# A hybrid layer on one core: the steady batch's steps written out in another order

## The reference

```python
x = x + mixer(layernorm(x))          # RWKV-6: token shift, low-rank mixes, r/w/k/v/gate, a scan over time
x = x + butterfly_ffn(layernorm(x))  # two learned butterfly transforms with a gelu between
x = x + block(layernorm(x))          # causal attention with 16 heads of 16 (RoPE), then a 4x gelu MLP
x = x + butterfly_ffn(layernorm(x))  # the same weights as above
```

## Time and profile before

| | |
|---|---|
| median of 3 runs | 1728.87 us (1727.68 to 1731.99) |
| the profiled execution | 1731.26 us |
| its span, first to last instruction | 1729.4 us |
| PE busy | 1634.0 us, 94% of the span |
| DVE busy | 951.8 us, 55% |
| ACT busy | 722.3 us, 42% |
| POOL busy | 671.0 us, 39% |
| mean granted TensorE clock | 0.981 of full speed |

### The profile page before, as it was taken

How to read it: one execution, slowest core, us unless ns; L and a number is a source line. 1 busy time by engine, 2 the same in 40 slices (tenths; PEclk the granted TensorE clock), 3 DMA queues, 4 the chain that set the end, 5 groups by cost and what they waited for, 6 DMA issues and landing times.

```text
span 1729.4 us, 47107 instructions
## 1 busy us (share of the span) xinstructions
PE 1634.0 (94%) x20436; PEld 1186.2 (69%) x20436; DVE 951.8 (55%) x1978; ACT 722.3 (42%) x1510; POOL 671.0 (39%) x851
## 2 busy tenths in 40 slices
PE   6579999999999999999999999999999999999998
PEld 3467468865688557884588746886478845777577
DVE  6864657356553657446573565636565365734621
ACT  4433462334632454234623346324552346333441
POOL 5633335343532426333362434424263242723110
PEclk9889999999999999999999999999999999999999
DMA  5110000000000000000000000000000000000000
GB/s 185 51 50 13 3 14 3 1 26 14 3 2 13 13 14 3 2 25 2 15 3 1 26 14 3 2 1 26 14 3 1 14 13 2 3 2 0 2 13 13
DMA packets 20413, 26.22 MB, mean 15 GB/s; under 512 B 1488, under 2 KB 18800, under 8 KB 20208
## 3 DMA queue, kind: packets, MB, share of 16 engines
q1 hardware_dynamic: 19872, 22.16, 3.9%
q0 software_dynamic: 336, 1.05, 0.2%
HBM read 19.01 MB, written 4.19 MB: 13 GB/s over the span
## 4 chain that ended last, share of the span: by engine, by line
PE 74%; DVE 13%; ACT 6%; issue 4%; POOL 1%; DMA 1%; SPq 0%; DVEq 0%; POOLq 0%; ACTq 0%
PE ring L1593 20%; PE ring L1607 18%; PE ring L1579 5%; PE ring L1760 4%; PE attn_out L1787 4%; PE ring L1539 4%; PE ring L1711 4%; DVE maxes L1334 3%; PE ring L1646 3%; PE ring L1733 2%; PE ring L1531 2%; PE ring L1616 2%; PE ring L1739 2%; DVE mix L1223 2%; DVE x_z_xb L1177 1%
## 5 line engine op out<-in xcount | busy, mean ns | idle before, releaser
L1334 DVE TENSOR_REDUCE maxes<-ring 128x2 f32<-128x1024 f32 (+5 forms) x290 | 197.5, 739 | 82.5 <-PE ring L1739 82.0
L758 POOL TENSOR_TENSOR rstd<-mean_var,eps_and_power 128x2 f32<-128x2 f32 x96 | 19.5, 203 | 468.6 <-DVE mean_var L1171 468.6
L1607 PE MATMUL ring<-w_down,big 128*128 128x256 f32 x784 | 175.9, 379 | 0.0
L1607 PEld LDWEIGHTS ring<-w_down,big 128*128 128x128 f32 x784 | 147.3, 190 | 19.6 <-issue 0.4
L810 POOL TENSOR_TENSOR big<-big,decay_blocks 128x256 f32<-128x256 f32 x192 | 141.7, 767 | 41.6 <-issue 36.8
L781 POOL TENSOR_TENSOR mix<-mix,z_t 128x512 f32<-128x512 f32 x80 | 85.8, 1101 | 119.2 <-DVE mix L1223 119.2
L1760 PE MATMUL ring<-big 32*64 32x128 f32 (+3 forms) x2048 | 125.6, 458 | 1.7 <-DVE big L1366 0.9
L1025 ACT ACTIVATE big<-ring,up_bias 128x256 f32<-128x256 f32 x196 | 82.3, 471 | 103.5 <-PE ring L1593 103.5
L1267 DVE TENSOR_TENSOR big<-big,decay_blocks 128x256 f32<-128x256 f32 x192 | 123.7, 670 | 1.0
L1593 PE MATMUL ring<-maxes,w_mlp 128*128 128x256 f32 x512 | 118.2, 385 | 0.0
L1593 PE MATMUL ring<-v,w_up 128*128 128x256 f32 x512 | 117.1, 389 | 0.0
(11 more groups left out here) (202 smaller groups left out, 3323.8 us busy)
## 6 DMA issues: line engine op xcount, KB each, us to landing
x_in<-in_x SPq DMA_DIRECT2D x8, 512.0 KB, 3.8
delta<-in_x SPq DMA_DIRECT2D x7, 512.0 KB, 3.9
out<-x_z_xb SPq DMA_DIRECT2D x7, 512.0 KB, 3.0
w_mlp<-in_wm SPq DMA_DIRECT2D x2, 1024.0 KB, 6.2
w_mlp<-in_w_exp_t SPq DMA_DIRECT2D x1, 1028.0 KB, 9.9
v_ones<-in_w_con SPq DMA_DIRECT2D x1, 1024.0 KB, 9.9
w_mlp<-in_low_up SPq DMA_DIRECT2D x1, 1016.0 KB, 6.7
w_attention<-in_low_down SPq DMA_DIRECT2D x1, 1016.0 KB, 8.2
```

The costliest lines, as they stand in the source:

```text
L1334: nc.vector.tensor_reduce(maxes[:, t % 2, qt, 32 * gs[0] + row:32 * gs[-1] + row + 1:32], banks[:, first:last, lo:hi], AX_X, ALU.max).then ...
L1607: ins = mm(ps[:, a * D:(a + 1) * D], gelu(b, tag, m, t)[:, a * P:(a + 1) * P], wd[:, m, :], start=(m == 0), stop=(m == NF - 1))
```

## The change

Only the list changes: `merged_steps` and the part of `attention_steps` that is used where a next batch exists (batches 0 to 6) become written-out lists. The steps are the same ones, and so are the instructions of each; the attention of the last batch and the list ahead of the first batch keep their order. In the diff, cut here to the steps that stand elsewhere than before:

```diff
 merged_steps
-("w", 0) ("w", 1) ("w", 2) ("w", 3) ("g",) ("wo", 0) ("wo", 1)
+("w", 0) ("w", 1) ("w", 2) ("g",) ("wo", 0) ("w", 3) ("wo", 1)
-("tree",) ("A", 0, 0) ("r", 3) ("A", 1, 0) ("zt", "M", 0) ("A", 0, 1) ("zt", "M", 1) ("A", 1, 1)
+("tree",) ("A", 0, 0) ("A", 1, 0) ("r", 3) ("zt", "M", 0) ("zt", "M", 1) ("A", 0, 1) ("A", 1, 1)
-("kt", 2) ("kt", 3) dn M 1 2, dn M 1 3 ("norm", "G", 1) ("xbg",) ("s", 0) ("zt", "G", 0) ("s", 1) ("s", 2)
+("kt", 2) dn M 1 2, dn M 1 3 ("kt", 3) ("zt", "G", 0) ("norm", "G", 1) ("xbg",) ("s", 0) ("s", 1) ("s", 2)
-("o", 0) ("norm", "N", 0) ("o", 1) ("norm", "N", 1)
+("o", 0) ("o", 1) ("norm", "N", 0) ("norm", "N", 1)
-up G 1 0 ("ogt", 0) ("ogt", 1)
+("ogt", 0) up G 1 0 ("ogt", 1)
-("zt", "F", 0) dn G 0 2, dn G 0 3 ("zt", "F", 1) up F 0 0, 0 1, 0 2, 0 3
+("zt", "F", 0) dn G 0 2, up F 0 0, dn G 0 3, up F 0 1, 0 2 ("zt", "F", 1) up F 0 3
-dn G 1 0 ("proj", 0, 0, 0) ... ("norm", "B", 1) ("z2", 1) ... ("half", 0, 1, "low") ... ("zt", "B", 1)
+dn G 1 0 ("z2", 1) ("proj", 0, 0, 0) ... ("norm", "B", 1) ... ("zt", "B", 1) ... ("half", 0, 1, "low")
 attention_steps, where a next batch exists
-("roundq", 0, "high") ("fold", 0, 1, "high")
+("fold", 0, 1, "high") ("roundq", 0, "high")
-("turn", 0) blend and mix 1 0, 2 0
+blend and mix 1 0, 2 0 ("turn", 0)
-("V", 0, "a") ("S", 1, "b") ("V", 0, "b")
+("S", 1, "b") ("V", 0, "a") ("V", 0, "b")
-("E", 0, "c") ("S", 1, "c") k 0 0, 0 1, 1 0 ("V", 0, "c") ... roundq 2, half 3 0, half 3 1 ("turn", 1) k 1 1 ("E", 1, "a")
+("E", 0, "c") k 0 0 ("S", 1, "c") ("V", 0, "c") k 0 1 ... roundq 2, half 3 0 ("turn", 1) k 1 0, 1 1 ("E", 1, "a") half 3 1
-k 2 0, 2 1 ("E", 1, "b") x5 3 0, 0 0, 4 0
+k 2 0, 2 1, x5 3 0, 0 0, 4 0 ("E", 1, "b")
-k 3 0, 3 1 ("V", 1, "c") ("turn", 2) x5 3 1, 0 1, 4 1 ...
+k 3 0, 3 1 ("turn", 2) x5 3 1, 0 1, 4 1 ... ("V", 1, "c")
-("E", 2, "a") ("divide", 1) ("S", 3, "a")
+("E", 2, "a") ("S", 3, "a") ("divide", 1)
-("E", 2, "b") ("V", 2, "a") ("S", 3, "b") ("V", 2, "b")
+("E", 2, "b") ("S", 3, "b") ("V", 2, "a") ("V", 2, "b")
-v 1 0 ("V", 2, "c") ("turn", 3) v 1 1 ("E", 3, "a")
+v 1 0 ("turn", 3) v 1 1 ("V", 2, "c") ("E", 3, "a")
-("V", 3, "a") ga 0 ("E", 3, "c")
+("V", 3, "a") ("E", 3, "c") ga 0
```

More of the change, by code:

```diff
@@ L69, in dn @@
     return [("dn", tag, t, q) for q in qs]
-def blend(*pairs):
-    return [(kind, n, c) for n, c in pairs for kind in ("blend", "mix")]
 def merged_steps(cur, old, new):
[L78 to L100, removed]
@@ L102, in later @@
+    o = [
[19 rows of a table added]
+        ("fold", 0, 0, "low"), ("half", 0, 0, "low"), ("roundq", 0, "low"), ("fold", 0, 1, "low"),
+        ("roundk", 0, "low"), ("zt", "B", 1), ("dn", "G", 1, 3), ("half", 0, 1, "low")]
     def later(step):
@@ L116, in halves @@
         return [("half", t, i, "all") for i in range(2)]
[L118 to L121, removed]
     o = [("proj", 0, 0, 1), ("proj", 0, 1, 1), ("rot", 0, 0, "high"), ("rot", 0, 1, "high")]
@@ L149, in attention_steps @@
         return [(b, *s) for s in o]
[L150 to L174, removed]
@@ new lines, in attention_steps @@
+    if b < 0:
+        o = [
+            ("xl", 0), ("xl", 1), ("x5", 1, 0), ("x5", 2, 0), ("blend", 1, 0), ("mix", 1, 0), ("x5", 1, 1),
+            ("x5", 2, 1), ("blend", 1, 1), ("mix", 1, 1), ("blend", 2, 0), ("mix", 2, 0), ("blend", 2, 1),
+            ("mix", 2, 1), ("wa",), ("k", 0, 0), ("k", 0, 1), ("k", 1, 0), ("k", 1, 1), ("k", 2, 0), ("k", 2, 1),
+            ("x5", 3, 0), ("x5", 0, 0), ("x5", 4, 0), ("blend", 3, 0), ("mix", 3, 0), ("blend", 0, 0), ("mix", 0, 0),
+            ("blend", 4, 0), ("mix", 4, 0), ("k", 3, 0), ("k", 3, 1), ("x5", 3, 1), ("x5", 0, 1), ("x5", 4, 1),
+            ("blend", 3, 1), ("mix", 3, 1), ("blend", 0, 1), ("mix", 0, 1), ("blend", 4, 1), ("mix", 4, 1),
+            ("v", 0, 0), ("v", 0, 1), ("v", 1, 0), ("v", 1, 1), ("ga", 0), ("ga", 1)]
+    else:
+        o = [
+            ("proj", 0, 0, 1), ("proj", 0, 1, 1), ("rot", 0, 0, "high"), ("rot", 0, 1, "high"),
+            ("fold", 0, 0, "high"), ("half", 0, 0, "high"), ("fold", 0, 1, "high"), ("roundq", 0, "high"),
+            ("half", 0, 1, "high"), ("roundk", 0, "high"), ("S", 0, "c"), ("vb", 0), ("xl", 0), ("S", 0, "a"),
+            ("clear_values",), ("xbo",), ("vb", 1), ("half", 1, 0, "all"), ("half", 1, 1, "all"),
+            ("roundq", 1, "all"), ("S", 0, "b"), ("xl", 1), ("x5", 1, 0), ("x5", 2, 0), ("blend", 1, 0),
+            ("mix", 1, 0), ("blend", 2, 0), ("mix", 2, 0), ("turn", 0), ("x5", 1, 1), ("x5", 2, 1), ("blend", 1, 1),
[3 rows of a table added]
+            ("V", 0, "c"), ("k", 0, 1), ("fold", 1, 0, "all"), ("fold", 1, 1, "all"), ("roundk", 1, "all"),
+            ("half", 2, 0, "all"), ("half", 2, 1, "all"), ("roundq", 2, "all"), ("half", 3, 0, "all"), ("turn", 1),
+            ("k", 1, 0), ("k", 1, 1), ("E", 1, "a"), ("half", 3, 1, "all"), ("divide", 0), ("S", 2, "a"),
+            ("k", 2, 0), ("k", 2, 1), ("x5", 3, 0), ("x5", 0, 0), ("x5", 4, 0), ("E", 1, "b"), ("blend", 3, 0),
+            ("mix", 3, 0), ("blend", 0, 0), ("mix", 0, 0), ("blend", 4, 0), ("mix", 4, 0), ("V", 1, "a"),
[7 rows of a table added]
```

## The result

| | before | after |
|---|---|---|
| median, this comparison | 1730.43 us (1727.68 to 1732.22) | 1685.15 us (1683.65 to 1686.45) |
| profiled execution, span | 1731.26, 1729.4 us | 1684.32, 1682.5 us |
| TensorE busy | 1634.0 us, 94% | 1594.4 us, 95% |
| mean granted clock | 0.981 | 0.986 |

The ratio is 0.9737, with an interval of 0.9715 to 0.9758. The forecast was 1702, its range 1692 to 1720: the sign was right, the size too small by 17 us, and the measured time lies outside the range.

What follows compares the result with a forecast made beforehand. TensorE was taken as the bound, busy 198.56 of 203.00 us; gains of 15.8 (attention), 8.05 (middle) and 3.0 (batch 0) sum to 26.9, taking the profiled 1731.26 to 1704.4, 1702 as a median; range 1692 to 1720.

Steps and rivals of the forecast that it cites:

- (b): Attention, k 0 0 ahead of S 1 c: covers its 0.5 wait for the rotated k's bank, gain 0.37 us a batch.
- (d): Attention groups t = 1 and 2, blends, maxima and S 3 b moved: gain 0.45 us a batch.
- (a): Attention, blends 1 0 and 2 0 ahead of shift 0: E 0 a waits for no bank, gain 0.6 us a batch.
- (c): Attention, S 2 a no longer waits 0.9 for the copy of k 1: gain 0.94 us a batch.
- (e): Attention groups t = 2 and 3, turn 3 behind v 1 0, E 3 c ahead of ga 0: -0.1 us a batch.
- (f): Middle, g's copies ahead of w 3, levels paired, kt 3 and s regrouped: gain 1.15 us a batch, 1.0 before up M.
- (g): Other moves, ogt 0 and zt F 1 among them: nothing in steady batches, 3.0 us in batch 0.
- only waits and neighbours change: Whole kernel: the instructions stay the same, even the number of maxima instructions.
- rival 1: Attention keeps its length, each wait that goes replaced by the next; (f) and (g) alone, 1718 us; chance 0.20.
- Rival 2: TensorE: every change of shape is worth the full 0.19 us, 9.0 more in all, 1693 us; chance 0.15.
- Rival 3: Attention slower: turns 1 to 3 each wait for late maxima, (a) to (e) lost, 1745 us; chance 0.04.
- The marks named ahead: Signs: E 0 a about 1.2, named waits gone, 0.5 wait at turn 3, batches 198.9 apart, batch 0's waits shrunk.

Runs made afterwards that it cites:

- e8: The new kernel with only k 0 0 put back behind S 1 c: 1693.79 us, ratio 0.9789 to the kernel before.
- e9: The new kernel with the first levels apart again (A 0 0, r 3, A 1 0, zt M 0, A 0 1, zt M 1, A 1 1): 1686.50 us, ratio 0.9744.
- e10: The new kernel with V 2 c moved ahead of turn 3: 1686.45 us, ratio 0.9744 to the kernel before.
- e4: The new kernel again, unchanged, beside the parts on one chip: 1690.28 us, ratio 0.9777 to the kernel before.

## Why the prediction was right in sign and too small

Of the profiled executions, 1731.26 and 1684.32, the difference is 46.9; the sum had 26.9. The other 20.0 come from five places. Two steps of the prediction failed. The steady terms were priced too low in every execution (1), and the clock was taken as equal in both kernels (2), which is the larger part in this pair and the smaller one on average.

1. **The steady terms, 1.17 a batch, 8.2.** (b), (d) and (a) were undersized, by 0.38, 0.27 and 0.20. In (b) the wait was priced from the waits view at 0.5 and costs 0.86 from start to start (e8). (c)'s own 0.94 came to 0.93, because it was worked out from start to start, as (b) should have been. In (d) the sum put two changes of shape at nothing, one of them between S and V. Group 0 shows what that one is worth: from projection to projection TensorE takes 795.38 - 790.73 = 4.65 before, with V 0 a, S 1 b, V 0 b, and 777.76 - 773.24 = 4.52 after, with S 1 b, V 0 a, V 0 b. That is 0.13 for one change, and with 0.10 for the other (e9) it makes 0.23 of the 0.27. Of (a), 0.07 is that the shift came 0.07 earlier than worked out, and 0.07 that S 1 a takes 1.41 and not 1.48. (e) came to 0.11 for -0.10, with the loss at turn 3 that was forecast: e10 wins 0.5 by undoing it. (f) was 1.24 for 1.00 up to first up M, since the wait of zt M 1 cost 0.84 and not 0.62 (e9).
2. **The clock, 11.9 in this pair, about 4 to 6 on average.** The sum has no term for it, though the page of before has 0.981 and the low stretches were in its trace. "Gain 0.94" counted the wait of S 2 a by its own length, without the low clock that can follow it. From 200 us on the kernel before has 27.2 us at the low level in its profile, the new one 3.4; each costs half its length. Three of the seven stretches stand behind S 2 a (5.1), one behind turn 0, one behind zt F 1, two in the last attention, whose steps are the same in both kernels. Much of it is this one execution's luck: another profile of the new kernel (e4) has 15 us at the low level there. In the later comparisons the 62 executions of before have a mean of 1729.4 at a clock of 0.9798, the 13 of after 1688.4 at 0.9829. Fitted within kernels 0.001 of clock is worth 1.2 us, which makes 3.8 of the 41.0 between the means clock; by half the time at the low level it would be 6.1. The other 35 to 37 are order, where the sum had 26.9.
3. **The last batch, 2.1.** (g) priced the wait of zt F 1 for batch 0, where no other work lies beside it. The last batch has the same wait, 2.82 at 1545.23, since no next batch fills it either. After, what is left there is 0.69 ahead of the first up F.
4. **Batch 0, 0.5.** Ogt gives 2.25 - 0.61 = 1.64 and zt F 1 2.81 - 0.92 = 1.89, the 1.7 and 1.9 that were worked out, of which 3.0 was taken.
5. **The bursts, -3.4.** In this profile two batches take 7.35 and 7.91 from A 0 0 to up M where the others take 5.46, 4.4 more in all; the kernel before has 1.0 above its own 6.70. No row of before showed such a wait at that size, and "only waits and neighbours change" left it out.

8.2 + 11.9 + 2.1 + 0.5 - 3.4 = 19.3. The 0.7 left isn't settled. Ahead of 200 us the new kernel has 44.4 us at the low level and the kernel before 37.5, and that is counted nowhere here.

The rivals: rival 1 (each wait hands on to the next) is out, though new waits of 0.25 to 0.4 did appear. Rival 2 gave the nearest number, 1693, with a price that is too high: a change between 128x128 and 128x32 costs 0.10 (e9), which is what the sum took for the six in (f), and not the 0.19 of the earlier trace rows. But it was right to count the four in the attention, which the sum put at nothing: at 0.10 to 0.13 each they are an estimated 2.8 to 3.6 us in seven batches. So the rule of the Trainium skill on draining (TensorEngine Tiling, Key Properties) agrees with e9 and with these rows. Rival 3 is out: only turn 3 waits, 0.42 of the forecast 0.5, and (a) and (c) held. The marks named ahead came true, E 0 a at 1.14, no wait for the rotated k, k 1 or norm M; only the period is shorter than the 198.9 in four of six batches, 198.1 in the undisturbed one.

Not tried: a cover for the 0.64 of wo 0. Which product could stand there without another wait is open.

## What to carry to other kernels

Price a wait from the start of the step to the start of the next, against the same step where it doesn't wait; the waits view gave 0.47 for 0.86. Count every change of the array's shape, those between small shapes too. Before a sum, list where TensorE's clock is low and what stands ahead of it: behind a wait of 0.85 among small products another 1.7 was lost, in one batch of three. And compare means over many executions, since one pair of profiles made 11.9 of what is 4 to 6. And look for a wait that a filled steady batch hides in the first and in the last batch, both.

## What the runs showed of the hardware

The 1.2 GHz level followed short waits: one of 0.85 in 9 of 28 attentions, and in none of 98 without it; waits of 1.83 to 2.34 in a burst of small products in 10 cases, and none of the burst's waits under 1.8. And in a burst of 128 products of 128x32 by 32 columns, 1.3 us long, TensorE can stand still for up to 2.34 us, at fixed places of the program, until 2.15 to 2.95 us after the start of a packet of kind instruction. A change of the array's shape costs 0.10 between 128x128 and 128x32 and 0.13 between 128x32 and 32x128.
